# POOL adds the values' constant to x, PE keeps it for eight router columns

## The chip, the cores and the metric

One core of one Trainium2 chip. The metric is the time of the kernel on the device in microseconds. The kernel before the change takes 430.78 us (median of three timed runs, 429.72 to 431.52). The engines are called as the profile calls them: PE (TensorE), PEld (its loads of weights), DVE (VectorE), ACT (ScalarE), POOL (GpSimd), SP (SyncE).

## The reference

Input x is 32 batches of 256 tokens of 128 values, all fp32. Two blocks follow one another, each with a residual and a layer norm without weights behind it.

```
W   = W_attn + lora_attn_A @ lora_attn_B          (384 x 128)
xa  = x W^T;  xa = batch-norm over all 8192 tokens, gamma, beta
q, k, v = xa
y   = softmax(causal(q k^T / sqrt(128))) v
y   = y W_proj^T (W_proj + lora_proj)^T
x1  = layernorm(x + y)
h   = ln(x1) * router scale + bias;  logits = h router_w^T + router_b
gates: the two largest of the softmax over 8 experts, made to sum to 1
out = sum over the two experts of gate * (gelu(ln_e(x1) W1^T + b1) W2^T + b2)
x2  = layernorm(x1 + out)
```

Batch norm needs mean and variance over all tokens, so nothing of the attention can start before all of x has been read.

## The kernel before, in words

The start: x arrives in `x_all`, one row of 128 values (plus columns for the router and for bookkeeping) per token, and as `xT`, the same transposed. PE sums the Gram matrix of x while it arrives; from that the batch norm's scale and shift follow, and the weights are folded: `MT` for the scores, and `wvvT` (144 columns) for the values. A value row goes through both projections, so what PE makes of a token is 8 columns (`E`) that x itself brings to the router's logits, and `VW` = 136 columns of the projected value: 8 for the router and 128 for the row. The shift of the batch norm makes a constant in these 136 columns, the same for all tokens: `cv`, a tile with the same row on all partitions.

Since the rows of a softmax sum to 1, the constant of the values can be added to the values before or to the result after attention. The kernel before adds it to the values on PE, in `start_v`: one bf16 matmul of `ones_b` (all ones) with `cv3` (three rows that hold the constant split into three bf16 parts, in the columns of the values of both tiles of a batch) opens the group in `bank[1]`, and the two fp32 products of `make_v` (one for each tile of 128 tokens) add to it.

The attention stage takes the 32 batches one after the other. Each engine has its list for one step k, written out by hand, and the engines meet at semaphores: PE (L818) makes z of the next batch (L726), counts ranks of an older one (L711, three short f16 matmuls), opens the banks (L731, L736), transposes the probabilities of the batch before (L761), makes the next values (L740) and scores (L749 to L751) and attends (L770 to L772). In steps 6 to 10 it folds one expert's w1 as well (L677, L678). ACT copies z, probabilities and values out of PSUM, takes the exponentials, and the roots of the layer norm; its copy of v has two parts (L965, L966): the router's 8 columns go to `x_all`, the 136 to `vs`. DVE takes the row maximum, adds the attended values to the row of x (the residual, L1291), takes its moments, and routes: logits, maxima, one-hots (`oh_all`), places in the queues. The first batches have a list of their own (`first_steps`), and the ranks of batches 1 and 2 are taken earlier than those of the others.

POOL (L566) writes every routed row to its two places in `queue1` with an indirect DMA per tile of 128 rows, 64 in all, a batch as soon as its gate and its places are there. `part_transfers` (L556) puts a memset of a tile that nobody uses, 128 x 384, ahead of each transfer, to keep them apart. Each transfer counts up `s_scat[0]` (batches 0 to 17) or `s_scat[1]`.

The expert stage takes 142 tiles of 128 rows, 71 for the first choice of expert, 71 for the second. SP (L444) loads the rows of the first tiles once the first 18 batches have been written (`s_scat[0]`) and DVE has set the table of tiles (`s_tab`); PE turns, multiplies by w1 (L880) and w2 (L895); DVE and POOL finish. `s_cv` says at 1 that `cv` is there and at 2 that `cv3` is complete; DVE waits for nothing of POOL in the attention stage.

Of the kernel before, what the change touches and what calls it, by code (L numbers as in the profile page):

```python
# [28 lines left out]
BF16 = mybir.dt.bfloat16  # L29
# [7 lines left out]
P = 128  # L37
# [51 lines left out]
def build(nc, x, x_t, wide, low, r_b, w1_t, b1_rows, w2_t, b2, out):  # L89
# [40 lines left out]
    with ExitStack() as ctx:  # L130
        def sb(name, shape, dt=F32):
            return ctx.enter_context(nc.sbuf_tensor(name, shape, dt))
# [107 lines left out]
        cv = sb("cv", [P, VW])  # L240
        cv3 = sb("cv3", [P, TPB * (E + VW)], BF16)
        cvp = sb("cvp", [P, 3, VW], BF16)
        rls_bc, rlb_bc = sb("rls_bc", [P, P]), sb("rlb_bc", [P, P])
# [232 lines left out]
        def _(pool):  # L476
# [78 lines left out]

            def part_transfers():  # L556

                pg.settle()
                pg.did(pool.memset(idle[:, 0:3, :], 0.0))  # L559

# [5 lines left out]
            def scatter(b):  # L566
# [5 lines left out]
                for t in range(TPB):  # L572
                    part_transfers()
                    own_wait(pool, s_own_pool)
                    pool.indirect_dma_start(  # L575
                        out=queue1, out_offset=bass.IndirectOffsetOnAxis(x_int[:, b * TPB + t, POS1:POS1 + 1], 0),
                        in_=x_all[:, b * TPB + t, DATA:DATA + W1], in_offset=None).then_inc(s_scat[b >= NB0], 16)
# [35 lines left out]
            def first_pass(j):  # L613
                if j + CARRY_AHEAD < N1:
                    carry(j + CARRY_AHEAD)
                send_on(j)

            BETWEEN = 3
            for b in range(NB):
# [21 lines left out]
        def _(pe):  # L641
# [85 lines left out]

            def start_v(b):

                wait(pe, s_vs, b)  # L730
                mm(bank[1][:, 0:TPB * (E + VW)], ones_b[:], cv3[:], start=True, stop=False)  # L731

            def start_scores(b):
# [3 lines left out]

            def make_v(b):
                for t in range(TPB):
                    last = mm(bank[1][:, t * (E + VW):(t + 1) * (E + VW)], xT[:, b * T + t * P:b * T + (t + 1) * P],  # L740
                              wvvT[:], start=False, stop=(t == TPB - 1))
                last.then_inc(s_v, 1)
# [43 lines left out]
            def first_steps():  # L786
# [11 lines left out]
                pe.wait_ge(s_cv, 2)  # L798
                start_v(0)
                make_v(0)  # L800
                make_z(2)
                start_scores(2)
                attend(0)
                start_v(1)
                make_v(1)
# [4 lines left out]
                attend(1)  # L810
                start_v(2)
                make_v(2)
                rank(0)
                scores(3, 1)
                start_v(3)
                make_v(3)

            def attend_step(k, q, use, known):  # L818
# [6 lines left out]
                if has[-1]:  # L825
                    start_v(ahead)
                    start_scores(ahead)
# [264 lines left out]
        def _(v):  # L1092
# [98 lines left out]
            def split_constant(n):  # L1191

                op(v.tensor_copy(cvp[:, n, :], cv[:]))
                pg.settle()
                op(v.tensor_copy(cv3[32 * n:32 * n + 1, :].rearrange("p (t c) -> p t c", t=TPB)[:, :, E:E + VW],
                                 cvp[32 * n:32 * n + 1, n, :].unsqueeze(1).to_broadcast([1, TPB, VW])))
                if n < 2:
                    op(v.tensor_tensor(cv[:], cv[:], cvp[:, n, :], ALU.subtract))
                pg.settle()

            split_constant(0)

# [16 lines left out]
            def residual(b):  # L1219
                v.wait_ge(s_y, b + 1)  # L1220
                pg.settle()
                for t in range(TPB):
# [39 lines left out]
            def first_steps():  # L1262
                row_max(0)
                for n in range(1, 3):
                    split_constant(n)
                v.sem_inc(s_cv, 1)
                row_max(1)
# [7 lines left out]
            def attend_step(k, q, use, known):  # L1275
# [11 lines left out]
                if has[2]:  # L1287
                    v.wait_ge(s_y, b2 + 1)
                    pg.settle()
                    for t in range(TPB):  # L1290
# [335 lines left out]
```

## Time and profile before

| | us |
|---|---|
| median of three timed runs | 430.78 |
| lowest and highest | 429.72, 431.52 |
| the profiled execution | 431.83 |
| its span, first to last instruction | 430.1 |

| engine | busy us | share of the span |
|---|---|---|
| PE | 408.5 | 95% |
| PEld | 390.8 | 91% |
| ACT | 323.7 | 75% |
| POOL | 321.0 | 75% |
| DVE | 282.9 | 66% |

The mean granted clock of TensorE is 0.985 of full speed. Busy times are those of one profiled execution; the ends of matmuls are modelled, so for PE the distance from one start to the next tells more than a duration.

### The profile page before, as it was taken

The page shows a single profiled execution, that of the slowest core. Times are in us where ns is not written, and L with a number is a line of the kernel's source. Part 1 is how long each engine was busy: PE and PEld are TensorE (multiplying, and loading weights), DVE is VectorE, ACT ScalarE, POOL GpSimd, SP SyncE. Part 2 cuts the span into 40 slices and gives each one's busy share as a digit, 9 for nine tenths or more (in the row PEclk, how much of TensorE's full clock was granted, in tenths as well). Part 3 has the DMA queues.
Part 4 walks back from the last instruction along what each step waited for, and adds up shares of the span by engine and source line. Part 5 has one row for each costly group of instructions (what it writes and reads, how often), then busy time and mean ns, then how long its engine had stood idle before and what let it go on. Part 6 is the DMA issues. An engine that isn't in the chain of part 4 may idle for free.

```text
span 430.1 us, 14555 instructions
## 1 busy us (share of the span) xinstructions
PE 408.5 (95%) x3490; PEld 390.8 (91%) x3490; DVE 282.9 (66%) x1612; ACT 323.7 (75%) x830; POOL 321.0 (75%) x606
## 2 busy tenths in 40 slices
PE   7998899999998999999999999999999999999980
PEld 7967787999887999999999999999999999999980
DVE  2446677899999677656555555446766666666663
ACT  1226788999988678877888888888888888888751
POOL 7000276888888888888887787748878888788885
PEclk9999999999999899999999999999999999999995
DMA  9999411111113532454543355542333333333211
GB/s 236 323 402 378 117 41 34 42 45 48 42 47 115 123 85 85 127 148 137 138 128 108 98 166 155 161 139 72 106 101 105 111 108 109 108 83 101 69 32 37
DMA packets 45490, 51.69 MB, mean 120 GB/s; under 512 B 6610, under 2 KB 37074, under 8 KB 45410
## 3 DMA queue, kind: packets, MB, share of 16 engines
q1 hardware_dynamic: 37312, 31.46, 27.0%
q0 software_dynamic: 7728, 18.51, 12.7%
q10 hardware_dynamic: 370, 0.80, 0.6%
q8 instruction: 33, 0.54, 0.6%
q14 instruction: 47, 0.39, 0.3%
HBM read 28.23 MB, written 21.72 MB: 116 GB/s over the span
## 4 chain that ended last, share of the span: by engine, by line
PE 65%; POOL 13%; issue 12%; DVE 5%; ACT 1%; DMA 1%; POOLq 0%; SPq 0%; DVEq 0%; ACTq 0%
PE bank L880 19%; PE bank L895 18%; POOL r_z L603 7%; POOL out L609 6%; PE bank L686 3%; PE bank L740 3%; PE bank L870 3%; PE bank L726 2%; PE bank L761 2%; PE bank L677 2%; PE bank L749 1%; PE bank L770 1%; PE bank L772 1%; PE bank L751 1%; PE bank L750 1%
## 5 line engine op out<-in xcount | busy, mean ns | idle before, releaser
L880 PE MATMUL bank<-xT 128*128 128x128 f32 x1136 | 152.1, 277 | 0.0
L895 PE MATMUL bank<-w2T,xT 128*128 x1136 | 150.2, 275 | 0.6 <-DVE yt L1476 0.6
L895 PEld LDWEIGHTS bank<-w2T,xT 128*128 128x128 f32 x1136 | 138.2, 192 | 0.8 <-issue 0.8
L880 PEld LDWEIGHTS bank<-xT 128*128 128x128 f32 x1136 | 138.7, 193 | 0.0
L932 ACT ACTIVATE xT<-w1T,zero_col 128x512 f32 x139 | 100.4, 722 | 41.2 <-issue 37.5
L1476 DVE TENSOR_TENSOR yt<-bank,b_bc 128x128 f32<-128x128 f32 x142 | 41.4, 291 | 92.7 <-PE bank L895 87.6
L609 POOL DMA_INDIRECT out<-xT,xg x71 | 75.9, 1069 | 17.1 <-issue 17.1
L596 POOL DMA_INDIRECT queue<-xT,xg x71 | 72.0, 1014 | 20.1 <-POOL idle L594 16.2
L1069 ACT ACTIVATE xT<-bank 128x512 f32<-128x512 f32 x142 | 82.0, 577 | 2.4 <-PE bank L880 2.4
L575 POOL DMA_INDIRECT queue<-x_all x64 | 62.2, 972 | 12.6 <-issue 7.9
L932 ACT ACTIVATE xT<-bank,one_col 128x128 f32<-128x128 f32 x142 | 52.1, 367 | 10.9 <-PE bank L870 4.8
L559 POOL MEMSET idle<- 128x384 f32 x64 | 27.7, 433 | 28.1 <-ACT x_all L1030 27.8
L603 POOL TENSOR_TENSOR r_z<-ve_z,neg_half 128x1 f32<-128x1 f32 x68 | 40.1, 589 | 7.2 <-DVE ve_z L1523 4.2
L1531 DVE TENSOR_SCALAR xT<-zt,mv_z,r_z 128x128 f32<-128x128 f32 x71 | 25.2, 355 | 6.9 <-POOL r_z L603 6.1
L1482 DVE TENSOR_SCALAR xT<-xg 128x128 f32<-128x128 f32 x71 | 26.0, 366 | 0.6 <-DMA xg<-queue 0.3
L1504 DVE SCALAR_TENSOR_TENSOR xT<-yt,xg 128x128 f32<-128x128 f32 x71 | 25.4, 357 | 0.2
L1510 DVE SCALAR_TENSOR_TENSOR zt<-yt,xg 128x128 f32<-128x128 f32 x71 | 23.8, 336 | 0.0
L740 PE MATMUL bank<-wvvT,xT 128*128 128x144 f32 x128 | 21.1, 288 | 0.0
L870 PE MATMUL bank<-ident,xT 128*128 128x128 f32 x71 | 19.6, 276 | 0.8 <-DVE xT L1482 0.8
L1515 DVE BATCH_NORM_STATS2 st_z<-zt 128x6 f32<-128x128 f32 x71 | 20.2, 284 | 0.1
L932 ACT ACTIVATE prT<-bank 128x384 f32<-128x384 f32 x32 | 15.7, 489 | 5.7 <-PE bank L761 4.6
L1291 DVE SCALAR_TENSOR_TENSOR x_all<-bank,rinv,x_all 128x136 f32<-128x136 f32 x62 | 19.2, 352 | 1.0
(238 smaller groups left out, 740.1 us busy)
## 6 DMA issues: line engine op xcount, KB each, us to landing
xg<-queue SPq DMA_DIRECT2D x71, 129.5 KB, 2.2
xg<-queue SPq DMA_DIRECT2D x71, 67.5 KB, 2.0
x_all<-x SPq DMA_DIRECT2D x16, 256.0 KB, 6.1
xT<-x_t SPq DMA_DIRECT2D x8, 512.0 KB, 9.9
w1r<-w_t SPq DMA_DIRECT2D x8, 256.0 KB, 5.8
w2T<-w_t SPq DMA_DIRECT2D x8, 256.0 KB, 11.5
queue<-xT,xg POOLq DMA_INDIRECT x71
out<-xT,xg POOLq DMA_INDIRECT x71
```

What stands on the lines that cost most here:

```text
L559: pg.did(pool.memset(idle[:, 0:3, :], 0.0))
L575: pool.indirect_dma_start(out=queue1, out_offset=bass.IndirectOffsetOnAxis(x_int[:, b * TPB + t, POS1:POS1 + 1], 0), in_=x_all[:, b * TPB ...
L596: pool.indirect_dma_start(out=queue2, out_offset=bass.IndirectOffsetOnAxis(xg_int[:, slot, POS2 - DATA:POS2 - DATA + 1], 0), in_=orow[:, s ...
L603: pool.tensor_tensor(r_z[:, at], ve_z[:, at], neg_half[:, 0:1], ALU.pow).then_inc(s_pw, 1)
L609: pool.indirect_dma_start(out=out, out_offset=bass.IndirectOffsetOnAxis(xg_int[:, slot, TOK2:TOK2 + 1], 0), in_=orow[:, slot, 0:P], in_off ...
L740: last = mm(bank[1][:, t * (E + VW):(t + 1) * (E + VW)], xT[:, b * T + t * P:b * T + (t + 1) * P], wvvT[:], start=False, stop=(t == TPB - 1))
L870: tr(bank[q % 2][:, 0:P], (orow if k < N1 else xg)[:, slot, 0:P], ident[:]).then_inc(s_gt, 1)
L880: last = mm(bank[2 + s][:, h * P:(h + 1) * P], w1c[:, (q - 1) % WR, h * P:(h + 1) * P], xgT[:, s, :], start=True, stop=True)
L895: last = mm(bank[4 + s][:, 0:P], hs[:, s, h, :], w2T[:, bass.ds(e, 1), h, :].rearrange("p a d -> p (a d)"), start=(h == 0), stop=(h == HC ...
L932: return act.activation(out_, in_, ACT.Identity, bias=bias)
L1069: act.activation(hs[:, s].rearrange("p h t -> p (h t)"), bank[2 + s][:], ACT.Gelu).then_inc(s_hs, 1)
L1476: v.tensor_tensor(yt[:, j % 2, :], bank[4 + j % 2][:, 0:P], b2_bc[:, bass.ds(e * P, P)], ALU.add).then_inc(s_ys, 1)
```

## The change

The 128 columns of the constant leave PE. POOL adds them to the rows of x in `x_all`, ahead of the residual: the first 18 batches (`ADD_FIRST`), 36 adds of 128 x 128, in one go as soon as `cv` is there, and then one add ahead of each transfer of batch b for batch b + 18, where the memset shrinks from 384 to 128 columns. From batch 14 on, with no batch b + 18 left, the memset is as before. A new semaphore, `s_xa`, counts the batches whose rows are done; DVE waits for it before each residual.

PE keeps the eight router columns: `cv3` shrinks to 8 columns, and `make_v` adds it behind each of its two fp32 products with a bf16 matmul of 8 columns, in place of the one with 288 columns that `start_v` issued per batch. The wait for the copy of the values (`s_vs`) moves from `start_v`, which stood ahead of `start_scores` and `turn_p`, to `make_v` behind them. DVE's three splits of the constant cover 8 columns instead of 136, and all three come ahead of `row_max(0)`.

```diff
-        cv3 = sb("cv3", [P, TPB * (E + VW)], BF16)
-        cvp = sb("cvp", [P, 3, VW], BF16)
+        cv3 = sb("cv3", [P, E], BF16)
+        cvp = sb("cvp", [P, 3, E], BF16)
+        s_xa = sem("s_xa")
...
-            def part_transfers():
-
-                pg.settle()
-                pg.did(pool.memset(idle[:, 0:3, :], 0.0))
+            ADD_FIRST = 18
+
+            def add_constant(b, t):
+                row = x_all[:, b * TPB + t, DATA:DATA + P]
+                return pool.tensor_tensor(row, row, cv[:, E:VW], ALU.add)
+
+            def add_to_batch(b):
+                for t in range(TPB):
+                    last = add_constant(b, t)
+                last.then_inc(s_xa, 1)
+
+            def part_transfers(b, t):
+
+                pg.settle()
+                later = b + ADD_FIRST
+                if later < NB:
+                    last = add_constant(later, t)
+                    if t == TPB - 1:
+                        last.then_inc(s_xa, 1)
+                    pg.did(pool.memset(idle[:, 0, :], 0.0))
+                else:
+                    pg.did(pool.memset(idle[:, 0:3, :], 0.0))
...
+            pool.wait_ge(s_cv, 1)
+            for b in range(ADD_FIRST):
+                add_to_batch(b)
             BETWEEN = 3
             for b in range(NB):
                 scatter(b)
...
-            def start_v(b):
-
-                wait(pe, s_vs, b)
-                mm(bank[1][:, 0:TPB * (E + VW)], ones_b[:], cv3[:], start=True, stop=False)
...
             def make_v(b):
+
+                wait(pe, s_vs, b)
                 for t in range(TPB):
-                    last = mm(bank[1][:, t * (E + VW):(t + 1) * (E + VW)], xT[:, b * T + t * P:b * T + (t + 1) * P],
-                              wvvT[:], start=False, stop=(t == TPB - 1))
+                    at = t * (E + VW)
+                    mm(bank[1][:, at:at + E + VW], xT[:, b * T + t * P:b * T + (t + 1) * P], wvvT[:], start=True,
+                       stop=False)
+                    last = mm(bank[1][:, at:at + E], ones_b[:], cv3[:], start=False, stop=True)
                 last.then_inc(s_v, 1)
...
                 if has[-1]:
-                    start_v(ahead)
                     start_scores(ahead)
...
             def split_constant(n):
 
-                op(v.tensor_copy(cvp[:, n, :], cv[:]))
-                pg.settle()
-                op(v.tensor_copy(cv3[32 * n:32 * n + 1, :].rearrange("p (t c) -> p t c", t=TPB)[:, :, E:E + VW],
-                                 cvp[32 * n:32 * n + 1, n, :].unsqueeze(1).to_broadcast([1, TPB, VW])))
+                op(v.tensor_copy(cvp[:, n, :], cv[:, 0:E]))
+                pg.settle()
+                op(v.tensor_copy(cv3[32 * n:32 * n + 1, :], cvp[32 * n:32 * n + 1, n, :]))
                 if n < 2:
-                    op(v.tensor_tensor(cv[:], cv[:], cvp[:, n, :], ALU.subtract))
-                pg.settle()
-
-            split_constant(0)
+                    op(v.tensor_tensor(cv[:, 0:E], cv[:, 0:E], cvp[:, n, :], ALU.subtract))
+                pg.settle()
+
+            for n in range(3):
+                split_constant(n)
+            v.sem_inc(s_cv, 1)
...
             def residual(b):
                 v.wait_ge(s_y, b + 1)
+                v.wait_ge(s_xa, b + 1)
                 pg.settle()
...
             def first_steps():
                 row_max(0)
-                for n in range(1, 3):
-                    split_constant(n)
-                v.sem_inc(s_cv, 1)
                 row_max(1)
...
                 if has[2]:
                     v.wait_ge(s_y, b2 + 1)
+                    v.wait_ge(s_xa, b2 + 1)
                     pg.settle()
```

`start_v` goes from PE's first steps too, in all four places.

## Rows read from the trace of the kernel before

**Rows 1.** The page's part 4, shares of the chain that ended last.
```profile
PE 65%; POOL 13%; issue 12%; DVE 5%; ACT 1%; DMA 1%; POOLq 0%; SPq 0%; DVEq 0%; ACTq 0%
```

**Rows 2.** The chain in order of time, 82.8 to 86 us: start, us, what.
```profile
82.83 0.43 PE bank L726 x2
83.27 0.07 PE bank L711 x3
83.33 0.13 PE bank L731
83.47 0.11 PE bank L736
...
85.76 0.43 PE bank L726 x2
```

**Rows 3.** PE's timeline, where four steps start; then a row of the waits.
```profile
76.48 0.59 PE L726 MATMUL bank<-xT,MT 128*128 128x256 f32 x2
...
79.75 0.59 PE L726 MATMUL bank<-xT,MT 128*128 128x256 f32 x2
...
112.06 0.59 PE L726 MATMUL bank<-xT,MT 128*128 128x256 f32 x2
...
124.83 0.59 PE L726 MATMUL bank<-xT,MT 128*128 128x256 f32 x2
...
PEld bank L711 <- DVE oh_all L1332: 3.0, 7, 0.5
```

**Rows 4.** The chain at 40 us: two products behind short f16 matmuls.
```profile
40.44 0.04 PE bank L711 x2
40.48 0.32 PE bank L749 x2
40.79 0.22 PE bank L750 x2
```

**Rows 5.** PE's timeline at 24.6 us, an 8-column matmul and what follows.
```profile
24.67 0.29 PE L697 MATMUL bank<-wvvT,wp 128*128 128x8 f32 x2
24.81 1.10 PE L677 MATMUL bank<-w1r,fold_l 128*128 128x512 f32 x2
...
25.96 1.02 PE L677 MATMUL bank<-w1r,fold_l 128*128 128x512 f32 x2
```

**Rows 6.** The chain at 42 us, where L731 waited.
```profile
42.42 0.30 PE bank L731
```

**Rows 7.** POOL: timeline, then groups of instructions (busy, mean ns, idle before).
```profile
3.96 0.29 POOL L515 TENSOR_SCALAR_AFFINE_SELECT ident<-ones 128x128 f32<-128x128 f32 x1
4.22 0.29 POOL L517 TENSOR_SCALAR_AFFINE_SELECT ident_b<-ones_b 128x128 bf16<-128x128 bf16 x1
...
49.90 0.42 POOL L559 MEMSET idle<- 128x384 f32 x1 [22.87 <-ACT x_all L1030]
...
L603 POOL TENSOR_TENSOR r_z<-ve_z,neg_half 128x1 f32<-128x1 f32 x68 | 40.1, 589 | 7.2 <-DVE ve_z L1523 4.2
L559 POOL MEMSET idle<- 128x384 f32 x64 | 27.7, 433 | 28.1 <-ACT x_all L1030 27.8
L594 POOL MEMSET idle<- 128x64 f32 x71 | 10.7, 151 | 0.3
```

**Rows 8.** Timelines: POOL's last transfer of batch 17, and SP's first loads of rows.
```profile
111.50 0.96 POOL L575 DMA_INDIRECT queue<-x_all  x1 [0.17 <-POOL idle L559]
...
132.37 2.77 SPq L435 DMA_DIRECT2D xg<-queue  x3
```

**Rows 9.** DVE's timeline, one instruction twice, about 314 us.
```profile
312.87 0.32 DVE L1531 TENSOR_SCALAR xT<-zt,mv_z,r_z 128x128 f32<-128x128 f32 x1
...
314.77 0.53 DVE L1531 TENSOR_SCALAR xT<-zt,mv_z,r_z 128x128 f32<-128x128 f32 x1
```

**Rows 10.** Timelines of DVE and PE about the first route.
```profile
39.63 0.19 DVE L1250 TENSOR_TENSOR oh_all<-iota_e,ix 128x32 f16<-128x32 f32 x1
...
40.27 0.17 PE L711 MATMUL bank<-oh_all,ones_h 128*128 128x16 f16 x1
```

More of the change, by code:

```diff
@@ L572, in scatter @@
                 for t in range(TPB):
-                    part_transfers()
+                    part_transfers(b, t)
                     own_wait(pool, s_own_pool)
@@ L798, in first_steps @@
                 pe.wait_ge(s_cv, 2)
-                start_v(0)
                 make_v(0)
@@ L803, in first_steps @@
                 attend(0)
-                start_v(1)
                 make_v(1)
@@ L810, in first_steps @@
                 attend(1)
-                start_v(2)
                 make_v(2)
@@ L814, in first_steps @@
                 scores(3, 1)
-                start_v(3)
                 make_v(3)
```

## The prediction, before the changed kernel was run

> **What bounds the kernel now.** I read the chain of work first, then the timeline of TensorE (PE) in the attention stage, then the waits there, then POOL's timeline. The chain that ended last lies on PE for 65% of the span, with POOL and the issue gaps behind it [rows 1]. In the attention stage (about 30 to 135 us, 32 batches) it lies on PE alone for long stretches: one batch after the other without a gap, 2.93 us from L726 to the next L726, and the instruction that the change removes, L731, is a piece of 0.13 us in it [rows 2]. So PE time per batch is path time here, as long as PE doesn't wait. The expert stage behind starts from the end of this one: its tables and its first rows are made by the last batches. I see no slack there that would swallow a later start, so what attention loses or gains goes to the end whole.
>
> Not every batch is bound by PE. The step from 76.48 us takes 3.27 us instead of 2.92, and the four from 112.06 to 124.83 take 3.19 each; the waits name VectorE (DVE) for the four: L711 waited 3.0 us in 7 waits for oh_all [rows 3]. In these five, some 0.2 to 0.3 us more or less on PE is not seen.
>
> **PE, part by part.** Removed per batch: L731, one bf16 matmul with 288 columns, 0.13 us [rows 2]; I use 0.12, the distance of its start to that of L736 in the steady steps. Added per batch: two bf16 matmuls of 8 columns against ones_b, each behind one fp32 product of make_v and each followed by another fp32 matmul with other weights. By columns they are nothing. But what follows is the question. Between short 16-bit matmuls a place costs about 0.02 to 0.03 us (three L711 take 0.07). Where a short one is followed by fp32 weights, the follower is late: after L711, L749 takes 0.32 us where L750, the same shape behind an fp32 matmul, takes 0.22 [rows 4]. The nearest shape is L697, fp32 with 8 columns: its two passes take 0.14 us to the start of L677, and the L677 behind it lasts 1.10 where the next one lasts 1.02, so 0.22 for two passes, 0.11 each [rows 5]. I read this as the fp32 weights of the next matmul (about 0.11 us to load), which a long matmul hides and an 8-column one doesn't. So each added matmul costs 0.11, not 0.03: 2 x 0.11 - 0.12 = +0.10 us per batch (0.095 by unrounded pieces: 0.025 for the place and 0.08 for the follower, twice, less 0.12). The ends: 0.03 each would give -0.07 per batch; 0.14 each, were the dependence on the columns just written to cost a little, +0.16.
>
> The skill has a rule by which it would come out the other way. The Trainium skill, TensorE: Matmul & The Clock Gate, section Back-to-back issue gap, gives a floor of about 25 ns for matmuls of 1 to 64 columns; alone, that would make it two times 0.025 against 0.12, a gain. The same page's section LDWEIGHTS gives about P/1.2 ns, 107 ns for 128 columns, which agrees with the 0.11 of the rows; the floor agrees only with the L711 that another 16-bit matmul follows.
>
> How many batches: from the step that begins at 53 us on there are 25 calls of make_v (batches 7 to 31), less the five steps that wait for others: 20 x 0.095 = **+1.9 us**. The steps with a fold of w1 (4.1 us) count: PE has no wait in them either.
>
> **The first batches.** make_v(0) starts some 0.06 sooner (its s_cv comes earlier, since all three splits are now 8 columns wide) and ends as before; make_v(1) is beside a wait for prT. In the first ordinary step, L731 waited for the copy of v of the batch before, up to 42.42 us, and turn_p stood behind it [rows 6]. With that wait moved to make_v, turn_p goes ahead and the step gains 0.3 to 0.4 us. Against it: in the next two steps the path runs L711, L740, then ScalarE's copy of v, exponentials, roots, then the route on DVE; L731 stands outside it there, so its removal gives nothing, and the two short ones cost 0.14 to 0.2 each. With the 0.15 on batch 4 and 0.02 on batches 2 and 3 the first seven batches come to about **+0.2 us**.
>
> **DVE.** Its splits shrink from 136 to 8 columns, but move ahead of row_max(0): three of them at some 0.4 us from 30.2 us on end at about 31.5, and row_max(0) could not begin before 31.77 anyway, when scores(0) was there. The 1 us they leave free behind it was beside PE. The new wait for s_xa: residual(0) came at 36.24 us, and adds 0 and 1 are done by 31; batch b needs its pair 2.9 us or more after the batch before, so POOL is ahead in the burst; batches 18 and up are added some 17 batches ahead of use. Nothing waits, if an add takes under 1.4 us. Behind a late residual there would be all of DVE's queue, s_yr and with it the next attend. 0 us.
>
> **POOL.** An add of 128x128 fp32 from SBUF is not in the trace. The nearest rows: a select with one input of 128 columns starts 0.26 us ahead of the next, and memsets of 384 and 64 columns take 0.433 and 0.151, so 0.88 ns per column [rows 7]. An add that costs as much as the select gives the lower end, 0.26; with the second input read after the first, 128 x 0.88 ns more, 0.37; the power of one column, 0.59 [rows 7], is my upper end. I take 0.36, near to the select with its second pass. The Trainium skill, GPSIMD Engine Reference, section Elementwise - side-by-side cycle accounting, prices a two-input element at about 2.6 cycles, which would be some 0.28 us for the columns beside the dispatch; the sum would not change.
> - The burst: 36 adds from about 30.1 us (s_cv) are done at 43, before the first scatter at 49.90, for which POOL idled 22.87 us [rows 7]. At 0.59 they end at 51.3, 1.4 us late, which the later waits for GE (27.8 - 22.9 = 4.9 us in all) swallow.
> - In 28 of the 64 transfers an add takes the place of 256 columns of memset: 0.36 - 0.23 = +0.13 us, 3.6 us in all. POOL works without a pause from about 80 us, so 1 to 2 us of it stay. SP needs the last of the first 18 batches only at the table, at 132.37 us, and it is issued by 111.50 + 0.96 [rows 8]: 19.9 us of cover. Were the cover gone, each us would go to the end. The second group of rows is read some 35 us after the last scatter. 0 us.
>
> **DVE against POOL.** Both read and write SBUF. Where POOL issued an indirect DMA, DVE's L1531 took 0.53 instead of 0.32 us [rows 9], so there is interference; DVE's tensor_tensor with two SBUF inputs against a POOL add isn't in the trace. In the burst the route of batch 0 (from 38.46 us) has four such instructions, and its oh_all was done 0.45 us before PE came to L711 [rows 10]. Bounds: nothing, or 4 to 6 times a whole add of 0.36 less the slack, 1.7 us. I take 0.2. Later there is an add only every 1.7 us and DVE is 0.25 us short of PE per batch: 0, at most 0.4 us in each of some seven batches.
>
> The Trainium skill, SBUF - State Buffer, section Who interferes with whom, calls the pair of ports an exclusive lock, and has a two-input DVE instruction block against a GpSimd instruction that reads SBUF. No row of this trace shows that pair; it speaks against the change and for the third rival below.
>
> **The sum.** 1.9 + 0.2 + 0.2 = +2.3 us on the profiled execution, 431.83 (span 430.1 and 1.7 around it), so 434.1; that execution is 1.05 above the median of the three timed runs, 430.78, so the forecast of the median is **433.1 us**.
>
> **Rivals.**
> - Cheap short matmuls (other side: faster). If the fp32 weights come in under the product before the short one, or the 0.08 us lie in something else than a load, each costs 0.03: 20 x -0.07 = -1.4, and the start gains 0.3: 429.1. It decides at 0.06 us per short matmul. For it: the three L711 at 0.07 us [rows 2]. Against it: the followers in [rows 4, 5] with their 0.08 to 0.10. Chance 0.16.
> - No change: the 2.3 are swallowed, because more steps than five lean on ScalarE and DVE, whose own work per batch is 2.7 us. 431 +- 0.5. Against it: no wait in the steady steps. 0.08.
> - The port: every two-input instruction of DVE waits behind an add, in the burst and up to 97 us: +1.7 and 7 x 0.3 on top: 436.5; half of it is likelier, 435. 0.14.
> - POOL is too slow. The cover of 19.9 us, the waits of 4.9 and 19.8 and the 6.4 of memset saved, 51 us, are used up from 0.80 us for each of the 64 adds; at 0.9 us the expert stage starts 6.6 us late, 440. Against it: every row of one column but the power. 0.04.
> - My forecast: 0.58.
>
> **Numbers.** A measurement of this kernel tells about 0.5%, 2.15 us, from no change; so faster is below 428.6, slower above 432.9, and my forecast lies at the edge. Of its 0.58, 0.33 lie above, 0.25 within. Slower 0.33 + 0.14 + 0.04 = 0.51; same 0.25 + 0.07 + 0.07 = 0.39; faster 0.10, most of it from the first rival. Its own range is 432 to 434.3; with the first rival below and half of the port above, 429.4 to 436.
>
> **What would show it.** Right: the steady step of PE at 3.01 to 3.02 us; the fp32 matmul behind each new one with 0.08 us more; batch steps from 112 us on still 3.2; the add at about 0.36 us from start to start; no wait of DVE for s_xa; first scatter near 50 us. Wrong: a steady step below 2.9 us; DVE's route at 38 us longer by over 0.5 us; a wait of SP for the scatters of the first group.

## The result, and the profile after

The changed kernel takes 441.70 us (median of 6 runs, 440.54 to 443.75); the kernel before took 431.05 beside it (429.72 to 431.84). The ratio is 1.0263, with a 95% interval of 1.0243 to 1.0284: 2.6% slower, where I had forecast 433.1 and a range up to 436.0. The direction was right, the size was not.

The page of the changed kernel: the span is 439.7 us (430.1 before), the profiled execution took 441.43. The chain of work that ended last, by engine, answers to [rows 1]; the clock row of the 40 slices has a 7 that before did not have.

```profile
PEclk9999799999999999999999999999999999999995
...
PE 49%; POOL 22%; issue 14%; DVE 5%; SPq 4%; DMA 3%; ACT 2%; POOLq 0%; DVEq 0%; ACTq 0%
```

The shares drew me to the late stages, and wrongly: from the start of the last batch's L748 (L726 before) to the end of the span, it takes 439.7 - 141.39 = 298.3 us, against 430.1 - 132.03 = 298.1. Nearly all of the 9.6 us is made in the attention stage, and the starts of `MT`'s matmul (one per batch) say where. Batch 0 starts at 29.30 us (29.41 before), batch 2 at 36.12 (34.45), batch 4 at 48.18 (41.69), batch 7 at 61.47 (53.23), batch 31 at 141.39 (132.03): 8.2 of the 9.4 us are there by batch 7.

Next to look at is DVE's timeline for that stretch: start, us, line, output<-input.

```profile
30.13 0.47 DVE L1209 CAST cvp<-cv 128x8 bf16<-128x8 f32 x1
30.63 0.33 DVE L1211 COPY cv<-cvp 1x8 bf16<-1x8 bf16 x1
...
33.48 0.29 DVE L1229 TENSOR_REDUCE nmax<-bank 128x1 f32<-128x128 f32 x1 [0.57 <-PE bank L772]
...
40.10 4.10 DVE L1256 TENSOR_TENSOR lg<-x_all 128x16 f32<-128x16 f32 x1
44.23 0.17 DVE L1259 TENSOR_TENSOR lg<-lg,r_bias 128x16 f32<-128x16 f32 x1
...
52.96 0.17 DVE L1256 TENSOR_TENSOR lg<-x_all 128x16 f32<-128x16 f32 x1 [3.77 <-ACT x_all L993]
```

Two things are wrong there. The splits, eight columns each, last 0.3 to 0.5 us, and row_max(0) (L1229) begins at 33.48 instead of 31.77. And one product of 128x16, the first logits', stands 4.10 us; the same line takes 0.17 one batch later. Beside it, POOL's timeline:

```profile
30.12 14.05 POOL L561 TENSOR_TENSOR x_all<-x_all,cv 128x128 f32<-128x128 f32 x36 [3.20 <-DVEq L1205]
57.41 0.45 POOL L561 TENSOR_TENSOR x_all<-x_all,cv 128x128 f32<-128x128 f32 x1 [13.24 <-ACT x_all L1046]
```

The 36 adds run from 30.12 to 44.17 us, 0.39 from start to start, and DVE's instruction ends with the last of them. The one behind it is ordinary. PE, meanwhile, has nothing to do, as its timeline shows, and after that it is slow:

```profile
45.44 0.20 PE L733 MATMUL bank<-oh_all,ones_h 128*128 128x16 f16 x1 [3.37 <-DVE oh_all L1268]
45.49 0.19 PE L733 MATMUL bank<-oh_all,before 128*128 128x32 f16 x1
45.52 0.77 PE L770 MATMUL bank<-xT,zT 128*128 128x128 f32 x2
...
48.18 1.20 PE L748 MATMUL bank<-xT,MT 128*128 128x256 f32 x2
...
50.86 0.47 PE L770 MATMUL bank<-xT,zT 128*128 128x128 f32 x2
```

The view by windows has the granted clock for it (columns: busy time and count for each engine, then PEclk, DMA share, GB/s):

```profile
42.00:45.40 3.40, 0.07 (x2) 0.00 (x0) 3.25 (x10) 0.47 (x2) 2.17 (x6) 0.74 1.17 265
45.40:50.00 4.60, 4.56 (x20) 4.02 (x21) 2.31 (x11) 0.95 (x3) 0.00 (x0) 0.50 0.51 125
```

After 3.4 us in which PE was busy 0.07 us, the granted clock is 0.50 for 4.6 us, that is the 1.2 GHz of its two levels: L748 lasts 1.20 us where [rows 3] have 0.59. In the kernel before, the same stretch was granted 1.00. So the late instruction on DVE is paid twice here: PE waits, and then runs at half speed. It isn't so each time: in the second experiment below (PE's part undone) PE pauses for 2.08 us at the same place, and the granted clock stays at 1.00.

The steady step is as forecast. This is one step of PE's timeline, the counterpart to [rows 2]:

```profile
94.15 0.59 PE L748 MATMUL bank<-xT,MT 128*128 128x256 f32 x2
...
95.09 0.41 PE L760 MATMUL bank<-wvvT,xT 128*128 128x144 f32 x2
95.34 0.17 PE L762 MATMUL bank<-cv,ones_b 128*128 128x8 bf16 x1
95.37 0.49 PE L760 MATMUL bank<-wvvT,xT 128*128 128x144 f32 x2
95.70 0.17 PE L762 MATMUL bank<-cv,ones_b 128*128 128x8 bf16 x1
95.72 0.47 PE L770 MATMUL bank<-xT,zT 128*128 128x128 f32 x2
...
97.17 0.59 PE L748 MATMUL bank<-xT,MT 128*128 128x256 f32 x2
```

97.17 - 94.15 = 3.02 us (forecast 3.01 to 3.02), and the L760 behind a short matmul lasts 0.49 instead of 0.41, 0.08 more, as read in [rows 4, 5].

On POOL, the groups that answer to [rows 7] (busy, mean ns, idle before):

```profile
L561 POOL TENSOR_TENSOR x_all<-x_all,cv 128x128 f32<-128x128 f32 x64 | 26.3, 432 | 20.9 <-ACT x_all L1046 17.1 <-DVEq L1205 3.2
L578 POOL MEMSET idle<- 128x384 f32 x36 | 15.7, 437 | 0.5 <-POOL pad_rows L537 0.2
```

The first scatter is at 58.34 us, after an add at 57.41 and its memset, where the first memset stood at 49.90 before.

### The profile page after: what moved, and what is told of

Same layout as the page of the kernel before. It is cut to its first block, busy times and chain, and to the rows that moved or that the text cites. A ratio compares the mean times of both kernels' runs of the same rounds, so it can differ in the third digit from the quotient of the medians.

```text
span 439.7 us, 14678 instructions
## 1 busy us (share of the span) xinstructions
PE 413.3 (94%) x3518; PEld 394.5 (90%) x3522; DVE 289.8 (66%) x1612; ACT 324.5 (74%) x830; POOL 340.7 (77%) x670
## 4 chain that ended last, share of the span: by engine, by line
PE 49%; POOL 22%; issue 14%; DVE 5%; SPq 4%; DMA 3%; ACT 2%; POOLq 0%; DVEq 0%; ACTq 0%
PE bank L896 10%; PE bank L911 10%; POOL r_z L622 8%; POOL out L628 8%; PE bank L760 4%; PE bank L748 3%; PE bank L708 3%; PE bank L770 2%; POOL queue L594 2%; PE bank L782 2%; PE bank L699 2%; PE bank L772 2%; PE bank L771 2%; PE bank L791 1%; PE bank L793 1%
## 5 line engine op out<-in xcount | busy, mean ns | idle before, releaser
L561 POOL TENSOR_TENSOR x_all<-x_all,cv 128x128 f32<-128x128 f32 x64 | 26.3, 432 | 20.9 <-ACT x_all L1046 17.1
L1547 DVE TENSOR_SCALAR xT<-zt,mv_z,r_z 128x128 f32<-128x128 f32 x71 | 23.7, 333 | 7.2 <-POOL r_z L622 6.4
L760 PE MATMUL bank<-wvvT,xT 128*128 128x144 f32 x128 | 25.5, 316 | 0.0
L760 PEld LDWEIGHTS bank<-wvvT,xT 128*128 128x128 f32 x128 | 20.1, 198 | 0.9
L948 ACT ACTIVATE zT<-bank,u_z 128x256 f32<-128x256 f32 x32 | 15.2, 474 | 7.1 <-PE bank L748 7.0
L1531 DVE BATCH_NORM_STATS2 st_z<-zt 128x6 f32<-128x128 f32 x71 | 20.2, 284 | 0.0
```

Of the source, the lines that this page charges most:

```text
L561: return pool.tensor_tensor(row, row, cv[:, E:VW], ALU.add)
L760: mm(bank[1][:, at:at + E + VW], xT[:, b * T + t * P:b * T + (t + 1) * P], wvvT[:], start=True, stop=False)
L948: return act.activation(out_, in_, ACT.Identity, bias=bias)
```

## The experiments

Four groups of kernels ran on four chips, each group beside the kernel before on its own chip. That took 430.1, 449.9, 443.7 and 440.0 us (medians, the last a single time), so only ratios, and the starts of batches up to 110 us (which agree between the chips within 0.4 us where the kernels agree), are compared across groups. The ratios of the kernels timed in rounds have intervals; those with a single time (marked so) are read for their timelines, and their total only roughly.

**PE's part alone.** No add on POOL, no wait for it; the rows lack the constant. DVE's small splits stay where the change put them, all three ahead of row_max(0).

```
-            pool.wait_ge(s_cv, 1)
-            for b in range(ADD_FIRST):
-                add_to_batch(b)
...
-                v.wait_ge(s_xa, b + 1)
```

> The changed kernel without POOL's adds and without DVE's waits for s_xa (the memsets ahead of the transfers are the 384 columns of before); the 128 columns of the constant are in no row of x. Theory P (the loss is a collision of DVE with POOL's burst of 36 adds in the first 15 us of the attention stage; the steady steps cost only their 0.1 us): 1.0 to 1.5 us over before, 432 to 432.6; the steady step of PE stays at 3.02 us and PE has no idle time over 1.1 us in the first batches. Rival Q (the 8-column matmuls and the moved wait for the copy of the values lose the time by disturbing the first batches): 438 or more, PE still idle for over 3 us ahead of the first ranks.

Measured: 432.34 us (431.97 to 434.23) against 430.08, ratio 1.0056 [1.0036, 1.0077]. Batch 31 starts at 134.08, 2.05 us later than before, batch 7 at 53.80 (+0.57). In the chain of waits its step is whole, 3.03 us of PE and no gap:

```profile
86.64 0.43 PE bank L745 x2
...
87.59 0.25 PE bank L757 x2
87.83 0.01 PE bank L759
87.84 0.35 PE bank L757 x2
...
89.67 0.43 PE bank L745 x2
```

The second L757 takes 0.35 in the chain and the first 0.25: the time of a short matmul stands in the one behind it. So the forecast's +2.1 us for PE is right in sum, and the rival of cheap short matmuls is out: it would have needed a step below 2.9. Of the +0.57 at batch 7, though, 0.43 are there at batch 2 already (34.88 against 34.45), and they are the splits': row_max(0) comes 0.57 us behind the last of them, at 32.24 instead of 31.77.

```profile
31.51 0.16 DVE L1208 COPY cv<-cvp 1x8 bf16<-1x8 bf16 x1
32.24 0.29 DVE L1226 TENSOR_REDUCE nmax<-bank 128x1 f32<-128x128 f32 x1 [0.57 <-DVE cv L1208]
```

**PE's part undone.** The constant is again one matmul of 288 columns that opens the group; `cv3` holds it for the router's columns only, POOL adds as in the change.

```
+            def start_v(b):
+                wait(pe, s_vs, b)
+                mm(bank[1][:, 0:TPB * (E + VW)], ones_b[:], cv3[:], start=True, stop=False)
```

> The changed kernel with the constant's matmul of 288 columns back at its old place and with its old wait (zeros in the value columns, the router's eight still from there); POOL's adds, the waits for s_xa and DVE's small splits as in the change. Theory P: nearly all of the loss stays, 8 to 10 us over before, 439 to 441; the logits' first tensor_tensor still lasts about 4 us, until the last of the 36 adds. Rival Q: 431 to 433.

Measured: 438.52 us (437.87 to 439.36), ratio 1.0189 [1.0160, 1.0218], just below the range expected. Batch 31 at 138.78 (+6.75). Its DVE timeline has the same mark, 2.82 us here because the instruction comes later into the run of adds, which ends at 30.47 + 14.05 = 44.52:

```profile
41.73 2.82 DVE L1263 TENSOR_TENSOR lg<-x_all 128x16 f32<-128x16 f32 x1 [0.21 <-ACT x_all L999]
```

The two parts add up: 2.05 + 6.75 = 8.8 us of the 9.4, and the larger one is POOL's.

**A memset between the adds.** Would an instruction on POOL that reads nothing let DVE in?

```
                     last = add_constant(b, t)
...
+                    pg.settle()
+                    pg.did(pool.memset(idle[:, 0, 0:8], 0.0))
```

> The changed kernel with a memset of 8 columns (a write without a read) and the wait for the one before it behind each of POOL's 36 adds of the burst; the burst is longer by 36 x 0.1 to 0.2 us. Theory P1 (DVE's two-input instruction is kept out because the next add of POOL always holds the reading port before it is let in; anything between two adds that doesn't read lets it in): the 4.1 us of the first logits shrink to below 0.8, PE's idle time of 3.4 us goes, 433 to 436 in all. Rival P2 (DVE is kept out as long as POOL has work queued, reading or not; it is let in at the end of the burst): the first logits last as long as the burst, now 4 us or more longer: 445 or more.

Measured: 443.27 us (442.03 to 445.11), ratio 1.0303 [1.0263, 1.0344]. DVE was kept out again, until 46.15, the end of the last memset (46.05 and 0.11):

```profile
42.03 4.12 DVE L1259 TENSOR_TENSOR lg<-x_all 128x16 f32<-128x16 f32 x1
```

So DVE didn't come in between two of POOL's instructions here, even where they change in kind. The total expected for this case, 445 or more, was too high, because the product came later (42.03) and so stood no longer than before.

**The run cut in four.** 8, 8, 4 and 16 adds, each piece behind a semaphore that comes when DVE has done a route (`s_cv` 2, then `s_oh` 1, 2, 3).

```
-            pool.wait_ge(s_cv, 1)
-            for b in range(ADD_FIRST):
+            pool.wait_ge(s_cv, 2)
+            for b in range(4):
                 add_to_batch(b)
+            pool.wait_ge(s_oh, 1)
+            for b in range(4, 8):
+                add_to_batch(b)
...
```

> The changed kernel with its burst cut into parts: POOL waits for DVE's splits (s_cv at 2), adds for 4 batches, waits for the first one-hots, adds for 4, waits for the second, adds for 2, waits for the third, adds for the other 8. Theory P: the splits take 1.3 us again, the first row maximum starts by 32 us, the first logits' instructions last 0.2 us, and the time is that of the PE part alone, 432 to 433.5, if the single adds between the transfers cost nothing. Rival R (the adds between the transfers cost DVE time in each batch): 3 us or more above the PE part alone.

Measured: 441.22 us (437.29 to 441.38), ratio 1.025 [1.0225, 1.0275], though the attention stage is as with PE's part alone: batch 31 at 133.95. The time was lost afterwards. The last piece, 16 adds, held the first scatter back to 58.72 us, POOL stayed behind by some 8 us, and the first rows that it hands on went out at 159.88 instead of 152.06. The waits of DVE from 140 to 215 us (total, times, longest):

```profile
DVE xT L1506 <- DMA xg<-queue: 10.2, 11, 2.7
```

Before, that wait was 0.3 us, once; in the changed kernel 5.1, five times. The slots that the tiles' rows are read into are freed by POOL's sends, SP waits for them (19.4 us in 6 waits here, 12.6 in 4 before), and after eleven late reads PE stood still 2.2 us once. In this profile, 435.6 - 133.95 = 301.7 us lie between batch 31 and the end, against 298.1 in the kernel before and 296.7 with PE's part alone, on the same chip: 3.6 to 5.0 us more. The profiled execution (437.29) is the fastest of the five; the others took 440.69 to 441.38, and for these 4 us more there is no profile. Both expectations put this kernel's loss, if any, elsewhere: in the attention stage.

**The run cut in three, two batches shorter.** 14, 12 and 6 adds; the steady adds begin with the first scatter.

```
-            ADD_FIRST = 18
+            ADD_FIRST = 16
...
+            pool.wait_ge(s_cv, 2)
+            for b in range(7):
+                add_to_batch(b)
+            pool.wait_ge(s_oh, 1)
+            for b in range(7, 13):
+                add_to_batch(b)
+            pool.wait_ge(s_oh, 2)
...
```

> All of the change, with the adds ahead of the steady steps cut in three: seven batches after the splits, six after the first batch's one-hots, three after the second's; two batches fewer ahead of the first scatter. Theory A (the loss beside PE's part is all DVE's: a two-input instruction kept out to the end of a run of adds, PE idle and then at the 1.2 GHz level): no run of adds meets the splits or the first logits, the attention is that of the kernel with PE's part alone (z of batch 31 near 134, first scatter near 50.5), total 432.5 to 434. Rival B (POOL's own lag of 0.21 us for each transfer starves the first expert tiles of rows): attention the same, but the wait for a tile's rows grows as it did with the four-part cut (DVE waited 10.2 us for rows eleven times), total 436 or more.

> The kernel with the adds in three gaps once more, to narrow its ratio to before. If only PE's part is left of the loss: 1.004 to 1.008 of before. If POOL's lag or the single adds cost more on top: 1.010 or more. If even PE's part is taken back somewhere: 1.000 to 1.003.

Measured: ratio 1.0014 [0.9963, 1.0065] the first time, 1.0031 [1.0004, 1.0058] the second, a little below the 1.004 to 1.008 expected if only PE's part were left, with an interval that reaches into it. From the second: the splits at full speed, the first logits' product at full speed, and POOL's adds in the gaps.

```profile
30.22 0.17 DVE L1215 CAST cvp<-cv 128x8 bf16<-128x8 f32 x1
...
38.86 0.17 DVE L1262 TENSOR_TENSOR lg<-x_all 128x16 f32<-128x16 f32 x1
```

```profile
31.79 5.51 POOL L561 TENSOR_TENSOR x_all<-x_all,cv 128x128 f32<-128x128 f32 x14 [4.78 <-DVEq L1224]
40.30 4.72 POOL L561 TENSOR_TENSOR x_all<-x_all,cv 128x128 f32<-128x128 f32 x12 [3.00 <-DVE oh_all L1274]
47.25 2.38 POOL L561 TENSOR_TENSOR x_all<-x_all,cv 128x128 f32<-128x128 f32 x6 [2.23 <-DVE oh_all L1274]
```

Batches 2 to 6 start within 0.01 us of those with PE's part alone, batch 7 0.51 later: the first single add (50.26) and the first scatter stand beside a route, whose L1265 takes 0.42 us instead of 0.17 and whose one-hots (L1274) take 0.47 instead of 0.19. The first scatter is at 51.18, and DVE has no wait for rows between 140 and 240 us. So all 64 adds are there and cost next to nothing up to there; what is left of the loss agrees with PE's part. Behind 110 us the starts spread (batch 31 at 135.56 here and at 139.40 in the first try, against 134.08 with PE's part alone on another chip), and without a profile of the kernel before on these chips that part can't be put down to a cause. POOL's own lag (transfers 1.75 and 1.80 us apart instead of 1.56 while it adds) starves nobody, and that rival is out.

**One short matmul per batch.** On top of the three gaps: the products of both tiles first, in one group, then one matmul of 2 x 8 columns.

```
...
-                    last = mm(bank[1][:, at:at + E], ones_b[:], cv3[:], start=False, stop=True)
+                both = bank[1][:, 0:TPB * (E + VW)].rearrange("p (t c) -> p t c", t=TPB)
+                last = mm(both[:, :, 0:E], ones_b[:], cv3[:].rearrange("p (t c) -> p t c", t=TPB), start=False,
+                          stop=True)
```

> As the kernel with the adds in three gaps, with PE's constant for the 2 x 8 router columns of a batch in one short matmul behind both products, all of it right for both tiles. With my price of 0.12 us of spacing for each short matmul: 0.12 us less in each steady batch (steady step 2.91 instead of 3.02), the attention 2 us shorter than that of the kernel with two short matmuls, total the same as before within 0.4%, on either side. Rival: the saved matmul was hidden by what follows, then no difference to the kernel with two.

Measured, beside the three gaps: ratio 0.999 [0.9962, 1.0019], no difference from before that can be measured, where the kernel with two short ones had 1.0031 in the same group. The step in PE's timeline:

```profile
96.89 0.59 PE L754 MATMUL bank<-xT,MT 128*128 128x256 f32 x2
...
97.83 0.66 PE L766 MATMUL bank<-wvvT,xT 128*128 128x144 f32 x4
98.32 0.17 PE L769 MATMUL bank<-cv,ones_b 128*128 128x16 bf16 x1
98.35 0.47 PE L778 MATMUL bank<-xT,zT 128*128 128x128 f32 x2
...
99.80 0.59 PE L754 MATMUL bank<-xT,MT 128*128 128x256 f32 x2
```

2.91 us, 0.11 less than with two: the price of a short matmul in front of fp32 weights, measured by taking one away. By batch 22 it leads the kernel with two by 2.4 us (102.71 against 105.14), by batch 31 by 1.5, where 2 were expected. It is by its median the fastest form with the adds on POOL, and no faster than the kernel before. An earlier form of it closed each product's group before the constant, which leaves other values in the router's columns and so sends tokens elsewhere:

> As the kernel with the adds in three gaps, and PE's constant for the router's 2 x 8 columns in one short matmul behind both products instead of one behind each. Theory A with my price of PE's part (0.12 us of spacing for each short matmul): 0.12 us a batch less in 20 steady batches, steady step near 2.90, total 1.5 to 2.5 us below the kernel with the adds in gaps, 430 to 431.5: the same as before. Rival: the second short matmul is hidden behind the loads of the scores that follow, then under 0.5 us less.

Its ratio, 0.9958 [0.9924, 0.9993], belongs to another distribution of tokens and I take nothing from it but the step, 2.91 us as well.

**What keeps DVE out.** Four questions on the 4.1 us, by six kernels with one profiled run each (single times). First, the 36 adds replaced by memsets of 384 columns, 0.37 us apart:

```
-                    last = add_constant(b, t)
+                    pg.did(pool.memset(idle[:, 3 * t:3 * t + 3, :], 0.0))
```

> The 36 adds ahead of the first scatter are replaced by 36 memsets of 384 columns, so the first 18 batches' rows lack the constant. If it is the reading of two operands on POOL that keeps DVE out: splits at their old durations, the first logits' instruction near 0.17 us instead of 4.1, z of batch 31 near 134 and about 433 in all. If any run of instructions on POOL does: the first logits' instruction still ends with the last memset and the total is above 438.

```profile
30.29 0.41 DVE L1211 CAST cvp<-cv 128x8 bf16<-128x8 f32 x1
30.73 0.34 DVE L1213 COPY cv<-cvp 1x8 bf16<-1x8 bf16 x1
...
39.83 0.17 DVE L1258 TENSOR_TENSOR lg<-x_all 128x16 f32<-128x16 f32 x1
```

448.65 us against 449.9. A run of writes doesn't keep the product out; it does slow most of the splits' copies and casts, which are 0.17 and 0.16 with POOL idle. That part of the expectation (splits at full speed) missed, and so did batch 31 near 134 us (140.63). So there are two effects: the splits' (adds or memsets will do it, about 0.2 us each time), and the long one, which needs the adds. This is as the Trainium skill has it, SBUF - State Buffer, section Who interferes with whom: two SBUF inputs on DVE contend with what reads on GpSimd and not with what only writes, while a copy or a cast can take both ports.

Second, three two-input adds on scratch tiles at 35 us in the changed kernel:

```
+                for n in range(3):
+                    op(v.tensor_tensor(probe[:, n, :], probe_in[:, 0, :], probe_in[:, 1, :], ALU.add))
                 residual(0)
```

> The changed kernel, with three two-input adds of 128x16 on scratch tiles on DVE between the inverse and the residual of batch 0, near 36 us, in the middle of POOL's run of adds; nothing else of DVE reads what they write. If every plain two-input instruction of DVE that comes while POOL's adds run back to back is kept out to the end of the run: the first of them stands until about 44.2 (8 us), and the residual, batch 1's values and all of the attention with it are 6 to 8 us later. If only the first logits' instruction is (because of x_all, or of the idle time ahead of it): each takes 0.2 to 0.5 us, and the total stays near 442.

```profile
35.54 0.85 DVE L1287 TENSOR_TENSOR probe<-probe_in 128x16 f32<-128x16 f32 x3
```

Those pass at 0.28 us each, 13 to 14 adds into the run (single time 456.06 against 449.9). The first logits' product behind them is kept out to the end all the same:

```profile
40.48 4.11 DVE L1258 TENSOR_TENSOR lg<-x_all 128x16 f32<-128x16 f32 x1
```

Third, operands or place: two products in the form of the logits' at 35 us, and two scratch adds right ahead of the logits'.

> The changed kernel with four more two-input instructions of DVE, 128x2x8 each, written to scratch: two products of columns of x_all with one of its columns spread over them (the form of the first logits' instruction) near 35 us, where three adds on scratch took 0.28 us each, and two adds on scratch tiles right ahead of the first logits' instruction near 40 us. If the place decides (what DVE and ACT do around 40 us): the products at 35 us pass in under 0.5 us each, and the first add at 40 us is the one that is kept out to the end of the run of adds near 44.5. If the operands decide (x_all on both sides, with a column spread): the first product at 35 us is kept out to the end (9 us), everything behind it is late by as much, and the adds at 40 us would pass.

```profile
35.27 0.48 DVE L1291 TENSOR_TENSOR probe<-x_all 128x16 f32<-128x16 f32 x2
...
41.63 2.75 DVE L1260 TENSOR_TENSOR probe<-probe_in 128x16 f32<-128x16 f32 x2
44.31 0.16 DVE L1261 TENSOR_TENSOR lg<-x_all 128x16 f32<-128x16 f32 x1
```

The operands don't matter: the scratch add that comes at 41 us is kept out as well (451.69 against 443.71). Fourth, three kernels on what is special there: a filler of two MAX8 ahead of it, so that DVE doesn't pause; a probe at 38.3 us behind a pause; and the run of adds moved, four adds behind the splits and 32 from 36.8 us on.

> The changed kernel with two MAX8 of 128x8 on scratch put between the wait for ACT and the first logits' two-input instruction of batch 0, so that DVE starts it right behind a running instruction and not after a pause of 0.15 us. If the pause decides whether POOL's run of adds keeps it out: it takes 0.2 to 0.5 us near 40.6 instead of 4.1, PE isn't idle for 3 us, the time is 3 to 5 us less than the changed kernel's. If the place in the run decides (more than some twenty adds behind): it still stands until about 44.2.

```profile
41.59 2.56 DVE L1261 TENSOR_TENSOR lg<-x_all 128x16 f32<-128x16 f32 x1
```

> The changed kernel with one two-input add on scratch on DVE behind the wait for PE's values of batch 0, near 38.2, after DVE paused for some 2 us, 20 adds into POOL's run. If the pause decides: it is kept out to the end of the run, 6 us, and the residual of batch 0 with it. If what goes on around 40 us decides: it passes in under 0.5 us, and only the first logits' instruction is kept out.

```profile
38.30 6.33 DVE L1243 TENSOR_TENSOR probe<-probe_in 128x16 f32<-128x16 f32 x1 [2.64 <-PE bank L795]
```

> The changed kernel with the first four adds behind the splits and the other 32 only when PE has made the values of batch 0, near 36.2, so that the run lasts from there to about 48.8 and the first logits' instruction comes some seven adds into it instead of 25. If the length of the run ahead decides: it takes under 0.5 us. If the pause ahead of it or the place near 39 decides: it stands until about 48.8, 9 to 10 us, and the whole attention is later by 5 us more than in the changed kernel.

```profile
38.95 0.24 DVE L1258 TENSOR_TENSOR lg<-x_all 128x16 f32<-128x16 f32 x1
39.23 0.33 DVE L1261 TENSOR_TENSOR lg<-lg,r_bias 128x16 f32<-128x16 f32 x1
...
46.32 2.99 DVE L1258 TENSOR_TENSOR lg<-x_all 128x16 f32<-128x16 f32 x1 [2.10 <-ACT x_all L995]
```

Single times 449.69, 453.89 and 447.28 us against 439.95. A pause right ahead isn't it: with the filler the product still stands to 44.15. The last kernel speaks for the length of the run so far: at 38.95 us the same instruction passes, since the run began 2.2 us ago, and the one of the next batch, 9.6 us into the run, stands until its end (49.28). By depth into a run of adds (time since its start, divided by 0.39), two-input instructions passed at 6 to 14 adds (this kernel at 38.95; the probes at 35.3 and 35.5; in the kernel cut in four, 3.1 to 5.1 us into its last piece, at 0.24 to 0.49 us each), and were kept out at 20 (38.30), 24 to 26 (46.32, 40.48, and the changed kernel's at 40.10) and 29 (41.63, 41.73, 41.59, 42.03). In the splits they passed at 2 and 4 adds too (0.15 and 0.38 us). So the depth fits every case, with a limit somewhere between 14 and 20 adds, but it isn't the only thing that does. Each instruction that was kept out also came after DVE had paused for 1.87 us or more at some point since the run began, and each one that passed came in a run in which DVE had not paused for more than 0.6 us. No two-input instruction comes late in a run without such a pause, or early in one behind it, so which of the two decides is not shown, nor why.

## Why the prediction was wrong

- **PE, +0.10 us per batch: right.** Step 3.02 us, follower +0.08, 0.11 per short matmul taken away, and 2.05 us in attention with PE's part alone against 2.1 forecast. That the sum fits so well is in part luck: the first batches cost +0.57 instead of +0.2 (0.43 of it the splits', see next; the step that was to gain 0.3 to 0.4 us went from 3.15 to 3.03), the rest +1.5 instead of +1.9.
- **The splits, 0 us: wrong.** I priced three at 0.4 us with POOL idle, and let row_max(0) follow at once. Even with POOL idle they end at 31.67 and row_max(0) comes 0.57 us behind, 0.47 late. Under POOL's adds, the last of their instructions starts at 32.57 and row_max(0) comes at 33.48, 1.7 us late; batch 2 starts 1.24 us later than with PE's part alone (36.12 against 34.88).
- **DVE against POOL, 0.2 us with an upper bound of 1.7: the step that failed.** The bound said that an instruction waits at most for one add. It waited for about eleven: 4.10 us. From batch 3 to batch 4 the changed kernel loses 4.8 us against PE's part alone (48.18 - 39.39 = 8.79, against 42.14 - 38.16 = 3.98), 3.9 of it this one instruction (4.10 instead of 0.17). The forecast's own sign of being wrong, a route at 38 us longer by over 0.5 us, is what happened. The rival named the port, had 0.14, and was priced by the same bound, so it ended at 436.5 and missed as well (its terms add up to 436.7: 430.8 + 1.9 + 0.2 + 1.7 + 2.1). And [rows 9] were no measure of an interference: POOL had an indirect DMA running beside both L1531, from 312.41 to 313.44 us and from 314.24 to 315.28, and one of them took 0.32 us even so.
- **What the wait brings with it: not in the prediction.** PE idle for 3.37 us, then the granted clock at 0.50: +1.1 us in the step of batch 4 (4.13 against 3.03), and +0.5 at batch 6, where the route's instructions run beside the first single add and the first scatter (L1259 0.41 instead of 0.17, oh_all 0.48 instead of 0.19).
- **The steady adds, 0: right** behind batch 7 (steps of 3.02 us as with PE's part alone). In all, 1.24 + 4.80 + 1.10 + 0.53 = 7.67 us by batch 7 beside PE's 0.57, of which 0.4 is taken back later.
- **POOL, 0.36 us for an add: nearly right** (0.39); 0.13 more per transfer was 0.19 to 0.24. The end of the burst (43) was at 44.17. "No wait for s_xa" held. But the cover of 19.9 us was read at the wrong place: the first wait for a late POOL is not SP's for the table but DVE's for the rows of the first pass, which a lag of 8 us already brings out (the kernel cut in four). In the changed kernel, whose whole attention came late as well, these waits were 5.1 us, and the stretch behind batch 31 was no longer than before (298.3 against 298.1).

So the loss is 2.6%: 0.6% PE's part with the moved splits, and 2% POOL's adds, nearly all of it the one run of 36. With the run cut in three the ratio to the kernel before is 1.0014 and 1.0031.

## What to carry to other kernels

Before giving an idle engine a long unbroken run of two-input instructions, ask what DVE has to do meanwhile: price not one of them but the whole rest of the run, and place it in short pieces in DVE's own gaps, each behind a semaphore. A bound for an unseen contention is the length of the other engine's queue, unless a row shows that the loser is let in between two instructions. And a pause of PE can be paid again in its clock, as the 3.37 us were here.

## What the hardware showed that I had not expected

- A two-input fp32 instruction of DVE (128x16) stood 2.6 to 6.3 us, to the end of POOL's run of 128x128 adds, when it came 20 or more adds into the run, after a pause of DVE in it; two-input instructions took 0.24 to 0.51 us when they came 6 to 14 adds in, without such a pause. Memsets of 8 columns between the adds didn't let it in. A run of memsets alone gave 0.17. The product of PSUM with a scalar of each row and SBUF (L1241, 0.63 for two) was never held.
- The Trainium skill, SBUF - State Buffer, section Summary: rules for kernel authors, lets the second one to issue block until the first finishes. The runs agree that it blocks and differ in how long: here over the rest of a run, about seven to sixteen adds (2.56 to 6.33 us), not over one of them.
- Small copies and casts of DVE (128x8 and 1x8) took 0.28 to 0.47 us beside POOL's adds and 0.33 to 0.41 beside its memsets (one of the six 0.17), 0.16 and 0.17 with POOL idle.
- A bf16 matmul of 8 columns ahead of fp32 weights costs PE 0.11 us per step (3.02 us with two, 2.91 with one), and one of 16 columns costs about as much as one of 288: the step is 2.91 us with it and 2.92 in the kernel before.
- After its pause of 3.37 us PE was granted 0.50 of its clock for 4.6 us. After pauses of 2.01 and 2.11 us in two of the probe kernels (the filler ahead, operands or place) it was granted 0.50 too, after one of 2.08 us with PE's part undone it kept 1.00.
